# Four-stage transformer block on one Trainium2 core: a new order of the work in the local-attention layers, with VectorE's cosine products ahead of its sum of squares

## The reference

```python
qkv = x @ Wqkv;  q, k, v = split(qkv, 3)              # 128 -> 3 x 1024
q = l2norm(q) * qs;  k = l2norm(k) * ksc              # sum of squares over each head
q = q*cos*scale + rotate_half(q)*sin*scale            # k the same with 1/scale
sim  = q @ [k of the window before, k of its own] * 8 # 64 keys for each token, masked
attn = softmax(sim)
x = x + (attn @ [v before, v own]) @ Wo
xn = layernorm(x) * g + b
a, gate = split(xn @ W1 + b1);  x = x + (a * gelu(gate)) @ W2 + b2   # inner width 341
```

## Time and profile before

| what | value |
|---|---|
| median of 3 runs | 7113.0 us (7106.45 to 7114.45) |
| the profiled execution's own time | 7104.39 us |
| its span in the trace | 7102.6 us |
| last stage in the trace, from and to about | 3000 to 7070 us |
| busy share of the span: PE, DVE, ACT, POOL | 76%, 64%, 49%, 44% |
| granted TensorE clock, mean of the span | 0.887 of full speed |

### The profile page before, as it was taken

The page is one execution under the profiler, slowest core; times in us unless marked ns, Lnnn a source line. Parts: engine busy times, 40 slices in busy tenths (PEclk is TensorE's granted clock), DMA queues, the critical chain, the costliest instruction groups (busy, mean ns, idle before and its releaser), DMA issues. The chain is left out here.

```text
span 7102.6 us, 149155 instructions
## 1 busy us (share of the span) xinstructions
PE 5396.8 (76%) x55030; PEld 3291.0 (46%) x55030; DVE 4579.1 (64%) x5698; ACT 3469.8 (49%) x5663; POOL 3105.5 (44%) x1391
## 2 busy tenths in 40 slices
PE   4736777187584848678888888888888888888886
PEld 3524444022121212245556555656565665656554
DVE  4352111342332414489998888888888888889995
ACT  0002222023131312266777677677776776777773
POOL 0000000000000000187777777777777777777773
PEclk8658888588696968899999999999999999999997
DMA  0000000300101010010001000100100010001001
GB/s 17 0 7 20 27 27 27 50 3 11 17 0 27 0 27 1 35 32 20 19 20 41 19 18 23 38 19 20 40 20 18 20 40 20 18 20 25 18 20 35
DMA packets 116571, 152.29 MB, mean 21 GB/s; under 512 B 28616, under 2 KB 67410, under 8 KB 114750
## 3 DMA queue, kind: packets, MB, share of 16 engines
q1 hardware_dynamic: 116448, 150.66, 9.4%
HBM read 63.67 MB, written 11.53 MB: 11 GB/s over the span
## 5 line engine op out<-in xcount | busy, mean ns | idle before, releaser
L1602 POOL TENSOR_TENSOR d_qk_swap<-d_qk_raw,d_rot 128x512 f32<-128x512 f32 x768 | 1329.0, 1761 | 13.5 <-ACT d_qk_raw L1313 13.4
L99 POOL TENSOR_TENSOR ln_post_rstd<-ln_post_var,neg_half 128x8 f32<-128x8 f32 x16 | 27.4, 1712 | 2918.2 <-DVE ln_post_var L80 2918.2
L1609 POOL TENSOR_TENSOR d_rnorm<-d_sq_clip,neg_half 128x32 f32<-128x32 f32 x192 | 1048.1, 5459 | 87.9 <-DVE d_sq_clip L1472 87.1
L866 DVE TENSOR_REDUCE c_mx<-c_ps 128x1 f32<-128x512 f32 (+3 forms) x768 | 417.3, 556 | 772.5 <-PE c_ps L737 768.6
L1454 DVE TENSOR_TENSOR d_qk_part<-d_qk_raw,d_rot 128x1024 f32<-128x1024 f32 x384 | 878.0, 2306 | 38.8 <-ACT d_qk_raw L1313 32.5
L834 ACT ACTIVATE c_pt<-c_ps 128x512 f32<-128x512 f32 (+1 forms) x640 | 354.5, 555 | 1116.6 <-PE c_ps L752 1114.7
L1592 POOL TENSOR_TENSOR d_probs_n<-d_probs,d_prec 128x1024 f32<-128x1024 f32 x192 | 545.0, 2839 | 626.3 <-DVE d_prec L1497 626.2
L1150 PE MATMUL d_ring<-d_wqkv,d_xin 128*128 (+1 forms) x1536 | 724.1, 612 | 71.4 <-ACT d_xin L1346 54.1
L1377 ACT ACTIVATE d_band<-d_own_t 32x512 f32<-32x512 f32 x768 | 482.2, 628 | 458.4 <-DVEq L1464 451.7
L766 PE MATMUL c_ps<-c_pt,c_vg 128*32 128x512 f32 (+3 forms) x1536 | 629.6, 507 | 4.7 <-DVE c_ots L871 4.7
L1238 PE MATMUL d_ff<-d_ot,d_wo 128*128 128x256 f32 x1536 | 389.2, 411 | 139.3 <-DVE x_all L1523 139.3
(11 more groups left out here) (259 smaller groups left out, 9952.1 us busy)
## 6 DMA issues: line engine op xcount, KB each, us to landing
d_band<-d_prev_t SPq DMA_DIRECT2D x576, 64.0 KB, 2.0
d_v_prev<-d_v SPq DMA_DIRECT2D x191, 128.0 KB, 2.3
b_w<-in_L_ffn_w SPq DMA_DIRECT2D x64, 256.0 KB, 3.4
d_band_prev<-d_prev_t SPq DMA_DIRECT2D x192, 64.0 KB, 1.9
d_wqkv<-in_L_ffn_Wqkv SPq DMA_DIRECT2D x6, 1536.0 KB, 9.0
c_kp<-c_k_scratch SPq DMA_DIRECT2D x30, 256.0 KB
c_qp<-c_q_scratch SPq DMA_DIRECT2D x24, 256.0 KB
d_rot<-in_rot_base SPq DMA_DIRECT2D x6, 1024.0 KB, 8.0
```

Of the source, the lines that this page charges most:

```text
L1602: mm = eng.tensor_tensor(qk_swap[:, which, :, out:out + hd], qk_raw[:, which, :, src:src + hd], rot[:, bass.ds(par, 1), which, 1, bass.ds( ...
L1609: eng.tensor_tensor(rnorm[:, :], sq_clip[:, :], neg_half[:, 0:2 * HEADS], ALU.pow).then_inc(rn_ready, 1)
```

## The change

The stage keeps its slots, its tiles and its arithmetic; what is done in which slot, and in what order, changes on all engines.

- `blocks` of a tile moves from slot n-1 of DVE to the beginning of the next slot. POOL's division moves from before the sine part to after the power, and works in place on d_probs, which now has two buffers.
- ACT's four band copies go; SP issues eight transfers a slot for the bands in place of four. v_prev has two buffers.
- DVE multiplies by both halves of the cosine in front of the sum of squares; d_hid and the residual of the feed-forward now stand ahead of both.
- ACT: the exponential stands at the end of each slot; the gates move from the end of the even slot into the odd one, behind `raw(1)`; the instruction that preloaded the Gelu table goes.
- PE: w2 moves behind the four `turn`; `attended` is the last or next to last step of its slot, after `values`.

The core of the diff:

```diff
 # SP
+                    if g:
+                        eng.wait_ge(blocks_ready, n - 2)
...
                         for w in range(4):
                             r = slice(32 * w, 32 * w + 32)
-                            to = band[u][32 * w - 32:32 * w, w, :, :] if w else band_prev[u][96:128, :, :]
+                            eng.dma_start(band[1 - u][r, w, :, :], own_t[r, :, :]).then_inc(band_ready, 16)
+                            to = band[1 - u][32 * w - 32:32 * w, w, :, :] if w else band_prev[1 - u][96:128, :, :]
                             eng.dma_start(to, prev_t[r, :, :]).then_inc(band_ready, 16)
 # ACT
+                    def gates():
...
+                        for at, (c, lo, w) in enumerate(FFO):
+                            eng.wait_ge(w1_ready, 3 * (k - 3) + at + 1)
+                            eng.activation(gate[0:w, c, :], ff_bank(c)[0:w, 0:FB], ACT.Gelu,
...
                     if a:
                         raw(0)
                         raw(1)
-                    if f and u == 1:
-                        exponent(n - 2)
+                        if u == 0:
+                            square(0)
+                    if late:
+                        gates()
                     if a:
-                        square(0)
                         raw(2)
                         raw(3)
+                        if u == 0:
+                            square(1)
...
-                        for w in range(4):
-                            r = slice(32 * w, 32 * w + 32)
-                            eng.activation(band[p][r, w, :, :], own_t[r, :, :], ACT.Copy)
-                        eng.drain().then_inc(own_ready, 1)
...
                     if s:
                         values()
...
-                        eng.activation(table_probe[:, :], keep[:, 0:1], ACT.Gelu)
...
+                        exponent(n - 1)
 # DVE
+                    if g:
+                        blocks()
                     if s:
                         eng.wait_ge(rn_ready, n)
...
+                    if f:
+                        total()
...
                     if a:
+                        cosine(0)
                         cosine(1).then_inc(cos_done, 1)
-                    if f:
-                        blocks()
                     if a:
                         squares()
 # POOL, now after the power
+                    if f:
+                        eng.wait_ge(rec_ready, n - 1)
+                        eng.tensor_tensor(probs[u][:], probs[u][:], prec[:, :].unsqueeze(2).broadcast_to((P, HEADS, 2 * WIN)),
+                                          ALU.mult).then_inc(pn_ready, 1)
```

More of the change, by code:

```diff
@@ L947, in local_transformer_stage @@
         v_sb = [sb(f"v{p}", [P, INNER]) for p in range(2)]
-        v_prev = sb("v_prev", [P, INNER])
+        v_prev = [sb(f"v_prev{p}", [P, INNER]) for p in range(2)]
         qt = sb("qt", [P, 8, P])
@@ L951, in local_transformer_stage @@
         smax = sb("smax", [P, HEADS])
-        probs = sb("probs", [P, HEADS, 2 * WIN])
+        probs = [sb(f"probs{p}", [P, HEADS, 2 * WIN]) for p in range(2)]
         psum_row = sb("psum_row", [P, HEADS])
@@ L1111, in _ @@
                 through(LAYERS - 1, False)
-                slot(TILES, 0, 2, True)
-                slot(TILES + 1, 1, 2, True)
+                for n in range(TILES, TILES + 3):
+                    slot(n, n % 2, n < TILES + 1, 2)
                 eng.wait_ge(v_carried, 16 * (TILES - 1))
@@ L1240, in slot @@
                         mm.then_inc(wo_ready, 1)
[L1241 to L1245, removed]
+                    if s and u == 0:
+                        values(0)
+                        values(1)
                     if s:
@@ L1250, in slot @@
                         eng.matmul(ff[:, 1, :], center[:, :], x1s[:, bass.ds(eng.snap(column(n - 5)), FB)], start=True, stop=True).then_inc(c_ready, 1)
[L1251 to L1254, removed]
+                    if s and u == 1:
                         values(0)
                         values(1)
+                    if g:
+                        attended()
                     if odd:
@@ L1305, in slot @@
                     a, s, f, g = live(0), live(1), live(2), live(3)
-                    odd, even = u == 1 and live(5), u == 0 and live(6)
+                    odd, late = u == 1 and live(5), u == 1 and live(7)
                     def raw(c):
@@ L1497, in total @@
                         eng.reciprocal(prec[:], psum_row[:]).then_inc(rec_ready, 1)
-                    if f and u == 0:
-                        total()
+                    if g:
+                        blocks()
                     if s:
@@ L1514, in slot @@
                                                      op0=ALU.add, op1=ALU.mult).then_inc(hid_ready, 1)
-                    if f and u == 1:
-                        total()
-                    if a:
-                        cosine(0)
                     if late:
@@ L1550, in slot @@
                         centred()
-                    if u == 1 and a:
-                        rotated()
                     if odd:
@@ L1570, in _ @@
             def _(eng):
-                for z in (v_prev[:, :], kt[:, :, 0:WIN], band[0][:], band[1][:]):
+                for z in (v_prev[0][:, :], v_prev[1][:, :], kt[:, :, 0:WIN], band[0][:], band[1][:]):
                     eng.memset(z, 0.0)
```

117 lines of the change are left out of this document (53 added, 64 removed).

## The result

The changed kernel takes 7350.9 us (median of 4 runs, 7345.4 to 7356.1) where the kernel before takes 7113.0: 1.0336 times as long, 95% interval 1.0318 to 1.0354, or 238 us more. I had 7260, with a range of 7100 to 7370. The direction and the ring that decides were right. The size fell 91 us short: the time lies inside the wide range, and outside the 7210 to 7310 that I gave the forecast itself.

What follows compares the result with a forecast made beforehand. A ring through ACT and PE was taken to set the period at 42.61 us against 41.07: 96 x 1.54 = 148 us on 7104.39 gives 7252, stated as 7260 us; range 7100 to 7370, the forecast's own 7210 to 7310.

Steps and rivals of the forecast that it cites:

- The deciding ring: Chain of steps through ACT and PE over a pair of slots, claimed to set the period at 42.61 us.
- the wait for w2: Sign on DVE: a wait of 3 us for w2 ahead of x_all; only 1.6 us would make the prediction wrong.
- Step 4: Even slot, from `turn(3)` through `attended` and d_ot to the end of w1, w1 taking 2.66 us: reaches 27.90 us.
- The rival on the clock: PE's clock falls further with longer, new waits: 2 us added, period 44.6, 7450 us; chance 0.12.
- a slot's clock below 0.9: Sign of a wrong prediction: PE's granted clock in either slot falls below 0.9.
- a transfer that `attended` waits for: Sign of a wrong prediction: `attended` on PE has to wait for a transfer.
- Bands at nothing: SP's eight band transfers instead of four, needed by `attended` 13 us later, were costed at nothing.
- the last rival: POOL's power blocks `rotated` (46.4 us period, 7620 us) or bands land 1 us late (7360 us); chance 0.05.
- The ring through DVE and POOL: The other chain over a pair of slots, claimed at 41.1 us, no different from the 41.07 of before.
- the pause ahead of `blocks`: DVE waits 1.3 us for POOL's division, which now stands behind the power.
- the handover of w2 to the residual: Odd slot, PE to DVE: w2 was counted at 1.6 us with handovers, its own time being 1.56.
- The rule on the ports: Skill's rule that DVE and POOL lock their port pair exclusively per instruction; claimed not to hold for POOL's power.

Runs made afterwards that it cites:

- The early group: Changed kernel with w1's 85-row matmul group moved in front of PE's wait for d_ot: 7199.1 us (1.013).
- the moved table load: Changed kernel with the Gelu table loaded behind the exponential of the even slot on ACT: 7248.8 us (1.0204).
- squares moved back to the front: Changed kernel with DVE summing the squares ahead of both cosine products again: 7353.1 us (1.0353).
- the filled gap: Changed kernel with two extra matmuls of w1's 85-row group before the wait for d_ot, overwritten afterwards: 7245.1 us (1.0201).
- the kernel with group, table and loads: Changed kernel with w1's 85-row group before the d_ot wait, even-slot Gelu load, and next layer's weight loads behind slot 6's bands: 7177.5 us (1.01).
- the last experiment: On top of the kernel with group, table and loads: one cosine product before the residual, even-slot squares between the cosine products: 7088.5 us (0.9975).
- the combination with the early exponential: Changed kernel with even-slot Gelu load, odd-slot exponential before d_ot, even-slot squares behind `turned`, w1's 85-row group before the d_ot wait: 7268.8 us (1.0224).
- the kernel with the early exponential: Changed kernel with the odd slot's exponential ahead of d_ot and the v copies on ACT: 7273.0 us (1.0237).

## Why the prediction was right in direction and short in size

**The deciding ring** was the one named. Counted from the end of d_sq_clip at 5015.49, d_ot starts after 7.00 us (predicted 7.00), `raw(0)` after 11.28 (11.35), `turned(0)` after 15.40 (15.47), `turn(3)` after 16.03 (16.2), `attended` after 20.67 (21.05), the next d_ot after 23.74 (24.12), w1 after 24.90 (25.24). Behind w1 the residual on DVE follows after 8.92 us (predicted 36.65 - 27.90 = 8.75) and the end of d_sq_clip after 14.75 (14.71). The worst steps are those from `turned(0)` to `turn(3)`, 0.1 us too long, and from there to `attended`, 0.2 us too long. The ring without the clock's loss is 42.2 us where I had 42.6. The early group and the moved table load each gave time back, and squares moved back to the front gave none; this is what shows the ring, not the agreement of the sums alone. Of its signs, the wait for w2, given as 3 us, is 3.20 in most pairs, and w1 waits for d_ot.

**Step 4, w1 at 2.66 us, failed.** It measured 4.30 in the pair shown and about as much in two thirds of the pairs: I took w1's duration from a row in which PE came to it at 2.4 GHz, and put a wait of about 1.1 us for d_ot right in front of it. The rival on the clock had this as an alternative to my ring; it came true on top of it, and in w1 alone. My reason against it was that no wait gets much longer than those of now. That was so, and the clock fell all the same. In the kernel before, the same instructions have this row of windows:

```profile
5052.50:5055.20 2.70, 2.64 (x12) 2.24 (x13) 2.51 (x2) 2.12 (x5) 2.70 (x1) 1.00 0.13 26
```

The wait in front of them is 0.90 us there, and 1.22 now. Of the signs that I gave for a wrong forecast, a slot's clock below 0.9 and a transfer that `attended` waits for, the second is seen once in each of four layers; the first was badly chosen: from 5023.7 to 5044.7, w1 included, the mean is 0.92, since w1's 4.3 us at 0.50 and 0.69 are a fifth of it, and yet the cost is there.

**Bands at nothing: wrong once a layer, in four of the six.** The 13 us between issue and need are there in an ordinary slot; I did not look at what else SP issues once a layer. The transfers' side of the last rival is worth 32 us, of which the wait itself explains 19.

**The sum.** The ring costs (42.17 - 41.07) x 96 = 106 us, the clock about 1.7 us in 54 of 92 periods, 96 x 54/92 x 1.7 = 96 us (106 by the filled gap), the bands 32: together 234 to 244, of 238 measured, which is as close as single effects with some 10 us of error each can tell. The forecast's 148 us was for the ring alone, so there it was 42 too much; the 130 us beside it were left out. The two errors have opposite signs. That the time still fell inside 7100 to 7370 is in part luck: by my own words that range left out most of the clock's rival, which came true.

**The ring through DVE and POOL**, predicted at 41.1, shows as a median of 41.7 where it decides, with periods from 41.1 to 41.7. In it, POOL's division takes 1.90 (1.91), the pause ahead of `blocks` is 1.26 (1.3), two free cosine products take 2.36 (2.4). What I had too small is the handover of w2 to the residual: w2 ends at 5009.22 and x_all starts at 5009.66, 0.44 later, where I had hardly any. From d_var_eps to `blocks` it is 0.68 instead of 0.57, and 1.14 in the pair shown of the kernel with group, table and loads (5033.82 to 5034.96). Where this ring decides, the order of DVE's work counts: the last experiment is worth 1.25% or 89 us there (1.01 to 0.9975). It makes two moves at once, a cosine product ahead of the residual and, in the even slot alone, the squares between the products. What each is worth, and so what the order of the title costs there, was not tried apart.

**The rule on the ports.** The rows before had spoken against a full lock by the power, and the changed kernel repeats it: POOL's power starts at 5035.37 and takes 5.43 us, DVE's addition of two SBUF tensors starts at 5036.53 and takes 2.28:

```profile
5035.37 5.43 POOL L1601 TENSOR_TENSOR d_rnorm<-d_sq_clip,neg_half 128x32 f32<-128x32 f32 x1 [0.18 <-DVE d_sq_clip L1474]
```

So `rotated` did not wait for it. But the power waits for DVE where DVE is first: the last experiment has 6.34 us behind a cosine product that had 1.05 us still to run, and in the changed kernel's first slots it takes 7.42 us behind a `rotated` with 2.14 us to run. The Trainium skill, page "SBUF — State Buffer", section "SBUF: two separate sides", calls the shared port pair an exclusive lock for the whole instruction, held by whichever engine starts first. The traces agree where DVE is first, and do not where the power is.

**What stays open.** Why only two thirds of the pairs have w1 at the low clock, though the rows show the same wait of 1.20 to 1.22 us in front of nearly all. The products with d_wo stand behind a wait of 1.57 us and ran at the full clock in nearly every pair of the changed kernel, and in a quarter of those with group, table and loads they did not. The longest periods, 6 of 92 before and 12 of 92 now, come at the same pairs of each layer: the first, in four layers, is the late bands' (48.4 to 50.5 us); in the sixth, before and now, DVE first multiplies the next layer's tables (L1438, 2.91 us at 4762.38); in the fourteenth, where the slots of a layer end, PE sits idle for 3.5 to 3.8 us, and what it waits for there the profile does not show. Why the combination with the early exponential is slower than the early group alone is shown only in so far as its pauses and the clock behind them are seen; which of its edits makes the pause was not tried.

## What to carry to other kernels

When the order of work is changed, walk every ring that the new order closes, the ones through in-order engines with little work most of all: ACT was 40% busy and set the period, because a table load, two copies and an exponential stood in front of what the next slot needed. Price a matmul behind a new wait at both clock levels, and if such a wait has to be, look first for matmuls that can go in front of it: here two moved lines were worth 152 us. And test the edit that the change is named after by itself; this one, taken back alone, moved nothing.

## What the runs showed of the hardware

- PE waited 1.22 us behind a stretch of full work at 1.00, and the next 1.8 us were granted 0.50 and the 2.5 after that 0.69. With work of 1.09 us put into the wait, w1's 128-row matmuls took 379 ns each throughout.
- The low clock is not tied to one instruction: in the first combination, transposes behind pauses of 2.63 and 0.76 us took 3.55 us at 0.57 instead of 2.00. Nor does the length of the pause alone decide: the same 1.22 us was followed by it in two thirds of the pairs, and 1.57 us ahead of d_wo in nearly none.
- d_sq_clip, 32 elements in each partition, took 0.88 us in the last experiment instead of 0.18. It ended at 5028.80, and POOL's three sine instructions beside it (from 5024.04, 4.72 us) at 5028.76. POOL's elementwise work held DVE up there. POOL's power held up none of DVE's work, `rotated` beside it took 2.28 to 2.29 us throughout; but DVE held up the power: with a cosine product running at its start it took 6.34 us, with a `rotated` 7.42, else 5.43.
- An ACT table load runs ahead of the wait of its activation: in the kernel with the early exponential it took 1.28 us from 5033.31, and the exponential then waited 0.38 us for DVE. There it cost next to nothing; behind work, as between the v copies and the exponential at 5024.51, it costs its full time.
